# Products that need a normalised chunk, made inside the normalisation's own block

## The chip, the cores and the metric

The kernel runs on one core of one Trainium2 chip. The metric is the time of one execution in microseconds on the device. Before the change it is 1138.36 us, the median of 3 runs (1136.8 to 1141.94).

## The reference

Two layers work on 2048 tokens (64 batches of 32) of width 128, in float32, with a context of 64 x 257 rows of 128. All of it is one chain of residual sums:

```python
x = x + _L0_xattn_ref(_layernorm(x, axis=-1), ctx_1024, ctx_1024, mask_Bx1x1xS2_fk0, ...)
x = x + _L0_attn_ref(_layernorm(x, axis=-1), L0_attn_Wq, L0_attn_Wk, L0_attn_Wv, ...)
x = x + _L0_ffn_ref(_layernorm(x, axis=-1), L0_ffn_router_w, L0_ffn_router_b, ...)
x = x + _L1_xattn_ref(ctx_1024, _layernorm(x, axis=-1), mask_BxS2_bk0, L1_xattn_Wq, ...)
x = x + _L1_attn_ref(_layernorm(x, axis=-1), ...)
x = x + _L1_ffn_ref(_layernorm(x, axis=-1), ...)
```

`_layernorm` takes the mean and the variance over the 128 features and returns `(x - m) / sqrt(v + eps)`. The first four modules matter here: a cross attention of 16 heads to the context, a self attention with a memory term, a router that picks two of eight experts for each token, and a second cross attention (16 heads of 64) in which the latents are normalised again with an affine and stand beside the context as keys and values.

## The kernel before, in words

The tokens lie transposed in `xT` [128 features, 2048 tokens], the normalised ones in `yT`. The stages run one after the other in `perceiver`, and every stage consists of blocks (`nc.Block()`): in a block each engine has its own program, joined to the others by semaphores, and at the end of a block all engines wait for each other (in the trace `PEq L172` and the like: an engine that waited at the block's end).

`layernorm` (L168 to L225) works on four chunks of 512 tokens. PE makes the mean of a chunk with a matmul by a matrix of 1/128 (L193), DVE subtracts it (L204), ACT squares (L219), PE makes the variance (L196), ACT takes logarithm and exponential for the inverse root (L222, L225), DVE multiplies (L208) and, where there is an affine, applies it (L211). PE's program order is two means, then variances and means in turn, and at the end ten filler matmuls whose result nobody reads (`occupied(core, 0, 10)`, L56), which run while DVE and ACT finish the last chunks. The means are in PSUM banks 0 to 3, the variances in banks 4 to 7.

The four calls and what stands behind each:

- `cross_attention_0`, ln0. A block in which PE makes the queries of four chunks (L285) and a small product of the last context column (L287), DVE copies them out with bias and scale (L294, L297) and POOL builds a table of heads (L270 to L277). Then the loop's block, whose first instruction on SP loads context (L310).
- `memory_attention_0`, ln1. A block in which PE makes queries and keys of four chunks (L610), DVE copies the eight banks out (L624) and makes a gate (L627 to L631), and POOL fills and selects several tables (L586 to L595). Then the loop's block (POOL L685, L681, L682).
- `experts_0`, ln2, whose SP program also loads the experts' weights (`fetch`). In the block behind it PE makes the router's logits of 16 tiles of tokens into bank 0 (L1189) and transposes the tokens into rows in banks 4 to 7 (L1192); POOL first fills eight rank planes (L1115), and DVE's first step on the logits (L1365) waits for them and for the logits. ACT copies the rows out (L1294), SP loads context units (L1036) and then stores the rows (L1081), and POOL gathers from them much later (L1106).
- `cross_attention_1`, ln3 with an affine and the second epsilon. Behind it SP loads four masks (L1510), stores the latents' rows and, once these have landed, loads the rows of keys for the first two batches (L1518). PE transposes the latents (L1658), makes the queries of the first group of four batches (`queries(-1, ...)`, L1599), then waits for POOL's copy of the latents into the keys (L1565) and for DVE's rows of latents (L1768, `lat_kept`), and starts the loop. ACT copies the queries out (L1681).

The loop of `cross_attention_1` runs over 64 batches in 8 turns of 8; a batch is four units of four heads. For a unit PE makes scores into bank 0 or 1 (L1609), DVE adds the mask and takes the maximum (L1726), ACT the exponential (L1688), DVE the reciprocal of the sum (L1732), POOL multiplies by it (L1555), DVE transposes (L1740). Behind every second batch PE makes the means of two batches from the transposed probabilities and the rows of keys (L1622) in banks 2 to 5. The order on DVE is `maximum(u)`, `invert(u - 1)`, `turn(u - 2)`.

## Time and profile before

| what | value |
|---|---|
| median of 3 runs | 1138.36 us (1136.8 to 1141.94) |
| the profiled execution | 1137.78 us, its span 1135.5 us |
| PE, DVE, ACT, POOL busy | 1001.3, 738.2, 734.7, 485.9 us |
| mean granted TensorE clock | 0.964 |
| ln0, ln1, ln2, ln3 begin at | 8.88, 260.86, 383.66, 549.09 us |

The profile is of one execution, with times from its span's start. In a row of its timeline stand the start, the length, the engine, the line of the kernel, the operation with its tiles, and in brackets how long the engine stood idle before it and what ended that. Rows of one kind that follow each other are merged with their count, and a float32 matmul counts as two instructions. An engine's name with a q (SPq, POOLq) is its queue.

### The profile page before, as it was taken

The page shows a single profiled execution, that of the slowest core. Times are in us where ns is not written, and L with a number is a line of the kernel's source. Part 1 is how long each engine was busy: PE and PEld are TensorE (multiplying, and loading weights), DVE is VectorE, ACT ScalarE, POOL GpSimd, SP SyncE. Part 2 cuts the span into 40 slices and gives each one's busy share as a digit, 9 for nine tenths or more (in the row PEclk, how much of TensorE's full clock was granted, in tenths as well). Part 3 has the DMA queues.
Part 4 walks back from the last instruction along what each step waited for, and adds up shares of the span by engine and source line. Part 5 has one row for each costly group of instructions (what it writes and reads, how often), then busy time and mean ns, then how long its engine had stood idle before and what let it go on. Part 6 is the DMA issues. An engine that isn't in the chain of part 4 may idle for free. (4 is left out here: it accounts for less than half of the span.)

```text
span 1135.5 us, 37923 instructions
## 1 busy us (share of the span) xinstructions
PE 1001.3 (88%) x13868; PEld 793.3 (70%) x13868; DVE 738.2 (65%) x2792; ACT 734.7 (65%) x1794; POOL 485.9 (43%) x883
## 2 busy tenths in 40 slices
PE   5799999987688769998899999999999998878864
PEld 2678888873677459887678888888888887323343
DVE  3578888875789578995476556556556553473376
ACT  3578888873578528885376766766756754564467
POOL 1122222213655026675066666766666765102042
PEclk9899999999799889999999999999999999998979
DMA  2443333310000455773365445445455442000001
GB/s 61 115 115 78 83 81 77 83 39 1 1 1 2 159 189 187 233 226 99 97 154 144 119 114 144 114 117 137 118 126 133 112 123 68 29 0 0 1 0 38
DMA packets 70699, 105.57 MB, mean 93 GB/s; under 512 B 12560, under 2 KB 50320, under 8 KB 70384
## 3 DMA queue, kind: packets, MB, share of 16 engines
q1 hardware_dynamic: 68080, 98.84, 32.3%
q0 software_dynamic: 2496, 5.12, 1.7%
q8 instruction: 75, 1.23, 0.5%
q14 instruction: 48, 0.39, 0.1%
HBM read 89.12 MB, written 14.79 MB: 92 GB/s over the span
## 5 line engine op out<-in xcount | busy, mean ns | idle before, releaser
L1688 ACT ACTIVATE d_p<-d_p,d_nmax 128x289 f32<-128x289 f32 x256 | 137.1, 539 | 128.3 <-DVE d_nmax L1726 127.5
L1555 POOL TENSOR_TENSOR d_p<-d_p,d_rtotal 128x288 f32<-128x288 f32 x256 | 169.3, 667 | 39.6 <-DVE d_rtotal L1732 35.0
L1726 DVE CUSTOM_DVE_ANT_0 d_p<-bank,d_low 128x289 f32<-128x289 f32 x256 | 109.7, 429 | 79.7 <-PE bank L1609 78.3
L1609 PE MATMUL bank<-x_keyT,d_q 128*128 128x289 f32 x512 | 155.1, 420 | 3.5 <-DVE d_nmax L1726 2.1
L1622 PE MATMUL bank<-d_pT,d_xr 32*128 32x128 f32 x4608 | 137.9, 273 | 1.4 <-ACT rows_out L1697 0.9
L445 ACT ACTIVATE a_p<-a_p,a_nmax 128x257 f32<-128x257 f32 x256 | 116.2, 506 | 33.7 <-DVE a_nmax L482 31.9
L1622 PEld LDWEIGHTS bank<-d_pT,d_xr 32*128 32x128 f32 x4608 | 131.6, 187 | 6.3 <-issue 2.1
L1740 DVE STREAM_TRANSPOSE d_pT<-d_p 128x288 f32<-128x288 f32 x256 | 119.2, 465 | 22.1 <-POOL d_p L1555 19.7
L482 DVE CUSTOM_DVE_ANT_0 a_p<-bank,a_low 128x257 f32<-128x257 f32 x256 | 93.8, 422 | 28.0 <-PE bank L395 26.5
L1609 PEld LDWEIGHTS bank<-x_keyT,d_q 128*128 128x128 f32 x512 | 82.3, 190 | 35.1 <-DVE d_nmax L1726 23.6
L353 POOL TENSOR_TENSOR a_edge<-a_vlast,a_p 128x32 f32<-128x32 f32 x64 | 15.7, 246 | 178.0 <-ACT a_p L445 165.2
L452 ACT ACTIVATE a_pT<-bank 128x512 f32<-128x512 f32 x128 | 69.7, 594 | 21.1 <-PE bank L404 20.6
L1572 POOL TENSOR_TENSOR d_a<-rows_out 128x512 f32<-128x512 f32 x64 | 80.1, 1274 | 7.2 <-ACT rows_out L1697 6.6
L1732 DVE RECIPROCAL d_rtotal<-d_total 128x1 f32<-128x1 f32 x256 | 40.5, 158 | 52.1 <-ACT d_p L1688 52.1
L1635 PEld LDWEIGHTS bank<-d_a,x_wvo 128*128 128x128 f32 x512 | 66.2, 192 | 9.0 <-POOL d_a L1572 2.8
L1599 PEld LDWEIGHTS bank<-yT,x_wqk 128*128 128x128 f32 x512 | 66.7, 192 | 6.4
L1635 PE MATMUL bank<-d_a,x_wvo 128*128 128x128 f32 x512 | 67.0, 275 | 2.6 <-POOL d_a L1572 2.6
L404 PE MATMUL bank<-ident,a_p 128*128 128x128 f32 x512 | 68.1, 277 | 0.0
L1599 PE MATMUL bank<-yT,x_wqk 128*128 128x128 f32 x512 | 67.0, 275 | 0.0
L404 PEld LDWEIGHTS bank<-ident,a_p 128*128 128x128 f32 x512 | 61.3, 144 | 6.6 <-issue 0.2
L417 PEld LDWEIGHTS bank<-a_v,a_pT 128*32 128x32 f32 x4096 | 42.3, 111 | 23.4 <-ACT a_pT L452 21.6
L1264 ACT ACTIVATE c_hs<-bank,c_w 128x128 f32<-128x128 f32 x156 | 44.6, 368 | 14.7 <-PE bank L1166 13.9
(344 smaller groups left out, 2183.4 us busy)
## 6 DMA issues: line engine op xcount, KB each, us to landing
d_xr<-key_rows SPq DMA_DIRECT2D x256, 144.0 KB, 3.2
d_low<-mask_low SPq DMA_DIRECT2D x64, 144.5 KB, 3.8
a_ctT<-in_ctxT SPq DMA_DIRECT2D x64, 128.5 KB, 2.1
a_low<-mask_low SPq DMA_DIRECT2D x64, 128.5 KB, 3.0
c_ct<-in_ctx SPq DMA_DIRECT2D x32, 256.0 KB
key_rows<-c_ct SPq DMA_DIRECT2D x32, 256.0 KB, 2.3
c_w<-in_L_ffn_w SPq DMA_DIRECT2D x8, 578.0 KB, 10.3
c_w<-expert_out SPq DMA_DIRECT2D x8, 256.0 KB, 4.9
```

What stands on the lines that cost most here:

```text
L404: ins = nc.tensor.transpose(TP[k][:, 128 * g:128 * g + 128], P[:, r % 2, g, 128 * k:128 * k + 128], core.ident[:])
L445: nc.scalar.activation(P[:, r % 2, g, :], P[:, r % 2, g, :], ACT.Exp, bias=nmax[:, r % 2, g:g + 1], scale=-1.0).then_inc(exp_made, 1)
L482: nc.vector.tensor_tensor_reduce(P[:, r % 2, g, :], S[g], low[:, r % RING, :], -1.0, 3.4e38, ALU.add, ALU.min, accum_out=nmax[:, r % 2, g: ...
L1555: nc.gpsimd.tensor_tensor(p, p, rtotal[:, b % 2, g:g + 1].broadcast_to([128, EDGE]), ALU.mult).then_inc(normed, 1)
L1572: nc.gpsimd.tensor_tensor(a[:, n // 4 % 2, :, n % 4, :], context_part[:, n % 2].rearrange("p j (g q) -> p (j g) q", g=GROUPS), latent_part ...
L1599: ins = nc.tensor.matmul(Q[:, 128 * h:128 * h + 128], wqk[:, 4 * r + h, :], latT[:, bass.ds((i * 2 + ahead) * 128, 128)], start=True, stop ...
L1609: nc.tensor.matmul(S[u % 2], q[:, b // 4, b % 4, 4 * g:4 * g + 4, :].rearrange("p h q -> p (h q)"), keyT[:, bass.ds(i * EIGHT + b, 1), :]. ...
L1622: ins = nc.tensor.matmul((OL if latents else O)[n % 2][j], xr[rows, n % 2, k, :], pT[rows, n % 4, :, 32 * k:32 * k + 32], start=(k == 0 or ...
L1635: ins = nc.tensor.matmul(OUT, wvo[:, h, :], a[:, ago % 2, 4 * (h % 4) + h // 4].rearrange("p b q -> p (b q)"), start=(h == 0), stop=False)
L1688: nc.scalar.activation(p, p, ACT.Exp, bias=nmax[:, b % 2, g:g + 1], scale=-1.0, accum_out=total[:, b % 2, g:g + 1]).then_inc(exp_made, 1)
L1726: nc.vector.tensor_tensor_reduce(P[:, b % 2, g, 0:KEYS], S[u % 2], low[:, b % 4, :], -1.0, 3.4e38, ALU.add, ALU.min, accum_out=nmax[:, b % ...
L1740: nc.vector.transpose(pT[:, b % 4, g, :], P[:, b % 2, g, 0:EDGE]).then_inc(turned, 1)
```

## The change

`layernorm` gets two arguments. With `follow` the ten fillers are left out and PE calls `follow(pe, c)` for each chunk, once that chunk is scaled (L208) or, where `shaped` is given, once the affine is applied (L211). The four callers give it: the queries behind ln0 and ln1, for each chunk four router products and four transposes behind ln2, and behind ln3, with its first chunk, the 16 matmuls of the first group's queries, now into banks 0 to 3.

```diff
@@ -194,7 +194,15 @@
                 if s >= 1:
                     pe.wait_ge(squared, before + s)
                     nc.tensor.matmul(var[:, s - 1, :], core.mean_w[:], chunk(sq, s - 1), start=True, stop=True).then_inc(var_ready, 1)
-            occupied(core, 0, 10)
+            if follow is None:
+                occupied(core, 0, 10)
+            else:
+                for c in range(NCH):
+                    if shaped is None:
+                        pe.wait_ge(scaled, before + c + 1)
+                    else:
+                        pe.wait_ge(shaped, c + 1)
+                    follow(pe, c)
 
         @block.vector
...
@@ -230,7 +238,14 @@
     nc = core.nc
     DH, GROUPS, RING = D // HEADS, 4, 4
     QUADS = BATCH // RING
-    layernorm(core, "ln0", core.xT, core.yT)
+    q_made = core.sem("a_q_made")
+
+    def ask(pe, c):
+        if c == 0:
+            pe.wait_ge(core.weights.a_loaded, 128)
+        nc.tensor.matmul(core.bank[:, c, :], core.weights.a["wq"][:], chunk(core.yT, c), start=True, stop=True).then_inc(q_made, 1)
+
+    layernorm(core, "ln0", core.xT, core.yT, follow=ask)
     with ExitStack() as own:
         sb = lambda n, s, dt=F32: core.sb(n, s, dt, own)
         sem = core.stage_sem
...
@@ -280,9 +295,6 @@
 
             @block.tensor
             def _(pe):
-                pe.wait_ge(w.a_loaded, 128)
-                for c in range(NCH):
-                    nc.tensor.matmul(core.bank[:, c, :], wq[:], chunk(core.yT, c), start=True, stop=True).then_inc(q_made, 1)
                 pe.wait_ge(w.edge_loaded, 16)
                 nc.tensor.matmul(core.bank[0:BATCH, 4, 0:128], w.ctx_last[:], wv[:], start=True, stop=True).then_inc(vl_made, 1)
...
-                pe.wait_ge(w_loaded, 128)
-                for n, w in enumerate((wq, wk)):
-                    for c in range(NCH):
-                        nc.tensor.matmul(core.bank[:, n * NCH + c, :], w[:], chunk(core.yT, c), start=True, stop=True).then_inc(q_made, 1)
+                for c in range(NCH):
+                    nc.tensor.matmul(core.bank[:, NCH + c, :], wk[:], chunk(core.yT, c), start=True, stop=True).then_inc(q_made, 1)
 
             @block.vector
             def _(dve):
...
+        LG = core.bank[:, 0, 0:128]
+        logit_made, rows_turned = core.sem("c_logit_made"), core.sem("c_rows_turned")
+
+        def route(pe, c):
+            if c == 0:
+                pe.wait_ge(w_loaded, 176)
+            for m in range(4 * c, 4 * c + 4):
+                ins = nc.tensor.matmul(LG[:, E * m:E * m + E], core.yT[:, 128 * m:128 * m + 128], router[:], start=True, stop=True)
+            ins.then_inc(logit_made, 1)
+            for m in range(4):
+                ins = nc.tensor.transpose(core.bank[:, 4 + c, 128 * m:128 * m + 128], chunk(core.yT, c)[:, 128 * m:128 * m + 128], core.ident[:])
+            ins.then_inc(rows_turned, 1)
+
+        layernorm(core, "ln2", core.xT, core.yT, room=(flat[:, 0:TOK], flat[:, TOK:2 * TOK]), fetch=fetch, follow=route)
         sem = core.stage_sem
...
@@ -1184,14 +1214,6 @@
                     ins = nc.tensor.transpose(TC[u % 2][:, 128 * m:128 * m + rows], ct[0:rows, slot_of(u), m, :], core.ident[0:rows, 0:rows])
                 ins.then_inc(turned, 1)
 
-            pe.wait_ge(w_loaded, 176)
-            for m in range(TILES):
-                ins = nc.tensor.matmul(LG[:, E * m:E * m + E], core.yT[:, 128 * m:128 * m + 128], router[:], start=True, stop=True)
-            ins.then_inc(logit_made, 1)
-            for m in range(TILES):
-                ins = nc.tensor.transpose(core.bank[:, 4 + m // 4, 128 * (m % 4):128 * (m % 4) + 128], core.yT[:, 128 * m:128 * m + 128], core.ident[:])
-                if m % 4 == 3:
-                    ins.then_inc(rows_turned, 1)
             pe.wait_ge(prod_loaded, 64)
             pe.wait_ge(gate_step, 1)
             products(0, (wqT, wkT))
...
@@ -1359,7 +1381,7 @@
                                           ALU.subtract, ALU.mult)
                 ins.then_inc(centred, 1)
 
-            dve.wait_ge(logit_made, 1)
+            dve.wait_ge(logit_made, NCH)
...
-        layernorm(core, "ln3", core.xT, core.yT, affine[:, 2:3], affine[:, 3:4], twice=True)
+        q_made, shaped = core.sem("d_q_made"), core.sem("d_shaped")
+
+        def ask(pe, c):
+            if c == 0:
+                for r in range(4):
+                    for h in range(4):
+                        ins = nc.tensor.matmul(core.bank[:, r, 128 * h:128 * h + 128], wqk[:, 4 * r + h, :], core.yT[:, 0:128], start=True, stop=True)
+                    ins.then_inc(q_made, 1)
+
+        layernorm(core, "ln3", core.xT, core.yT, affine[:, 2:3], affine[:, 3:4], twice=True, follow=ask, shaped=shaped)
         latT, lat_rows = core.yT, core.out
 
```

In `cross_attention_1` the transposes of the latents move behind the first two scores, on DVE the rows of latents (L1768 before) behind the first two maxima, and the wait for them from the loop's start to the first means. POOL's copy of the latents into the keys comes in two parts, of the first 8 batches and of the other 56; PE waits for the second at the second turn.

```diff
-                nc.gpsimd.tensor_copy(keyT[:, :, CTX - 1:EDGE], latT[:].rearrange("p (b q) -> p b q", b=BATCH)).then_inc(latents_placed, 1)
+                for part in (slice(0, EIGHT), slice(EIGHT, BATCH)):
+                    nc.gpsimd.tensor_copy(keyT[:, part, CTX - 1:EDGE], latT[:].rearrange("p (b q) -> p b q", b=BATCH)[:, part]).then_inc(latents_placed, 1)
                 nc.gpsimd.memset(lasts[:], 0.0).then_inc(cleared, 1)
 
...
+                    if n == 0:
+                        pe.wait_ge(lat_kept, NCH)
                     if n % 2 == 0 and n >= 2:
                         pe.wait_ge(o_copied, 2 * n)
                     for k in range(BLOCKS):
...
+                def latent_rows():
+
+                    for m in range(TILES):
+                        ins = nc.tensor.transpose(core.bank[:, 2 + m // 4, 128 * (m % 4):128 * (m % 4) + 128], latT[:, 128 * m:128 * m + 128], core.ident[:])
+                        if m % 4 == 3:
+                            ins.then_inc(lat_turned, 1)
+
                 def body(i, first, last):
                     for b in range(EIGHT):
+                        if i == 1 and b == 0:
+                            pe.wait_ge(latents_placed, 2)
                         scores(i, b, 0, first)
                         scores(i, b, 1, first)
+                        if first and b == 0:
+                            latent_rows()
                         if not (last and b >= 4):
                             queries(i, b)
...
 
-                for m in range(TILES):
-                    ins = nc.tensor.transpose(core.bank[:, 2 + m // 4, 128 * (m % 4):128 * (m % 4) + 128], latT[:, 128 * m:128 * m + 128], core.ident[:])
-                    if m % 4 == 3:
-                        ins.then_inc(lat_turned, 1)
-                for r in range(4):
-                    queries(-1, 4 + r)
                 pe.wait_ge(latents_placed, 1)
-                pe.wait_ge(lat_kept, NCH)
                 unrolled(TURNS, body)
                 for r in range(3):
...
+                def latent_rows():
+
+                    for c in range(NCH):
+                        dve.wait_ge(lat_turned, c + 1)
+                        nc.vector.tensor_tensor(lat_rows[:, 4 * c:4 * c + 4, :], core.bank[:, 2 + c, :].rearrange("p (m d) -> p m d", m=4),
+                                                cx.media[:, 1, :].unsqueeze(1).broadcast_to([128, 4, 128]), ALU.subtract).then_inc(lat_kept, 1)
+
                 def body(i, first, last):
                     for u in range(UNITS):
                         b, g = divmod(u, GROUPS)
                         maximum(i, u, first)
+                        if first and u == 1:
+                            latent_rows()
                         if b % 4 == 0 and g == 1 and i * EIGHT + b >= 12:
                             project(i, (b - 12) // 4)
                         if not (first and u < 1):
```

PE's program from the last variances of ln0 to the first scores' block. The names: `ln_sq` the squares, `wa_wq` the query weights. Before:

```order
L196 MATMUL bank<-ln_sq,mean_w 128x512 x2
L56 MATMUL bank<-ident,mean_w 128x128 x10
L172 UNCONDITIONAL_BRANCH
L281 UNCONDITIONAL_BRANCH
L285 MATMUL bank<-yT,wa_wq 128x512 x4
L287 MATMUL bank<-wa_wv,wa_ctx_last 64x128
L266 UNCONDITIONAL_BRANCH
```

and now:

```order
L196 MATMUL bank<-ln_sq,mean_w 128x512 x2
L246 MATMUL bank<-yT,wa_wq 128x512 x4
L172 UNCONDITIONAL_BRANCH
L296 UNCONDITIONAL_BRANCH
L299 MATMUL bank<-wa_wv,wa_ctx_last 64x128
L281 UNCONDITIONAL_BRANCH
```

The fillers (L56) are gone and the four query products stand in their place, ahead of the block's end (L172); of the next block's PE program only the small product is left.

PE's program at the end of ln3 and the opening of the second cross attention; `x_wqk` are the query weights, `d_q` the queries, `x_keyT` the keys. Before:

```order
L196 MATMUL bank<-ln_sq,mean_w 128x512 x2
L56 MATMUL bank<-ident,mean_w 128x128 x10
L172 UNCONDITIONAL_BRANCH
L1589 UNCONDITIONAL_BRANCH
L1658 MATMUL bank<-ident,yT 128x128 x16
L1599 MATMUL bank<-yT,x_wqk 128x128 x16
L1609 MATMUL bank<-x_keyT,d_q 128x289 x2
L1599 MATMUL bank<-yT,x_wqk 128x128 x4
L1609 MATMUL bank<-x_keyT,d_q 128x289 x4
```

and now:

```order
L196 MATMUL bank<-ln_sq,mean_w 128x512 x2
L1504 MATMUL bank<-yT,x_wqk 128x128 x16
L172 UNCONDITIONAL_BRANCH
L1621 UNCONDITIONAL_BRANCH
L1638 MATMUL bank<-x_keyT,d_q 128x289 x2
L1676 MATMUL bank<-ident,yT 128x128 x16
L1628 MATMUL bank<-yT,x_wqk 128x128 x4
L1638 MATMUL bank<-x_keyT,d_q 128x289 x4
```

The 16 query matmuls (L1599, now L1504) moved ahead of the block's end, and the 16 transposes (L1658, now L1676) behind the first two scores.

DVE's program at the same place; `rows_out` holds the latents' rows, `d_p` the probabilities. Before:

```order
L1716 UNCONDITIONAL_BRANCH
L1768 TENSOR_TENSOR rows_out<-bank,x_media 128x512 x4
L1726 ISA d_p,d_nmax<-bank,d_low 128x289
L1726 ISA d_nmax 128x1
L1726 ISA d_p,d_nmax<-bank,d_low 128x289
L1726 ISA d_nmax 128x1
L1732 RECIPROCAL d_rtotal<-d_total 128x1
L1726 ISA d_p,d_nmax<-bank,d_low 128x289
L1726 ISA d_nmax 128x1
L1732 RECIPROCAL d_rtotal<-d_total 128x1
```

and now:

```order
L1751 UNCONDITIONAL_BRANCH
L1761 ISA d_p,d_nmax<-bank,d_low 128x289
L1761 ISA d_nmax 128x1
L1761 ISA d_p,d_nmax<-bank,d_low 128x289
L1761 ISA d_nmax 128x1
L1794 TENSOR_TENSOR rows_out<-bank,x_media 128x512 x4
L1767 RECIPROCAL d_rtotal<-d_total 128x1
L1761 ISA d_p,d_nmax<-bank,d_low 128x289
L1761 ISA d_nmax 128x1
L1767 RECIPROCAL d_rtotal<-d_total 128x1
```

The four steps on the latents' rows stand behind the first two maxima, ahead of the first reciprocal.

## Rows read from the trace of the kernel before

**Rows 1.** The profile's page, its span, then busy time of each engine (first section).

```profile
span 1135.5 us, 37923 instructions
...
PE 1001.3 (88%) x13868; PEld 793.3 (70%) x13868; DVE 738.2 (65%) x2792; ACT 734.7 (65%) x1794; POOL 485.9 (43%) x883
```

**Rows 2.** Timeline, end of ln0, query block, loop's start: start us, length us, engine, line, operation.

```profile
18.51 2.39 PE L56 MATMUL bank<-ident,mean_w 128*128 128x128 f32 x20
...
21.20 3.67 PE L285 MATMUL bank<-yT,wa_wq 128*128 128x512 f32 x8 [0.30 <-PEq L172]
...
22.41 3.25 DVE L294 TENSOR_SCALAR a_qT<-bank,wa_bias 128x512 f32<-128x512 f32 x4 [1.63 <-PE bank L285]
...
25.57 0.27 DVE L297 TENSOR_TENSOR a_vl<-bank,wa_bv 64x128 f32<-64x128 f32 x1
...
26.12 0.33 SPq L310 DMA_DIRECT2D a_ctT<-in_ctxT  x1
```

**Rows 3.** Instructions of line 294, DVE's copies of the queries: count, ns min/median/max.

```profile
L294 DVE TENSOR_SCALAR a_qT<-bank,wa_bias x4: 751/751/751, 22.4 to 24.9; 128x512 f32<-128x512 f32 x4
```

**Rows 4.** Timeline, the block behind ln1: POOL's tables, DVE's copies, the next block.

```profile
272.19 0.10 POOL L590 MEMSET b_own_head<- 128x4 f32 x1 [20.68 <-SPq L577]
...
272.47 0.31 DVE L620 COPY b_norm<-wb_norm_col 64x1 f32<-64x1 f32 x2
...
278.45 0.46 POOL L586 TENSOR_SCALAR_AFFINE_SELECT b_key_scale<-b_key_scale 128x4 f32<-128x4 f32 x2
...
280.48 0.15 DVE L631 TENSOR_SCALAR wb_gate<-wb_gate 128x1 f32<-128x1 f32 x1
...
280.90 0.95 POOL L685 MEMSET b_vb<- 128x1024 f32 x1 [1.99 <-POOLq L577]
```

**Rows 5.** Timeline, end of ln2 and the start of the router's block.

```profile
393.53 2.39 PE L56 MATMUL bank<-ident,mean_w 128*128 128x128 f32 x20
...
396.18 0.45 POOL L1115 MEMSET x_keyT<- 128x16 f32 x8 [32.61 <-POOLq L172]
...
399.78 1.94 PE L1192 MATMUL bank<-ident,yT 128*128 128x128 f32 x16
...
399.97 0.29 DVE L1365 TENSOR_TENSOR x_keyT<-bank,wc_router_b 128x128 f32<-128x128 f32 x1 [4.16 <-PE bank L1189]
```

**Rows 6.** Timeline, end of ln3 and the opening of the second cross attention.

```profile
557.80 2.39 PE L56 MATMUL bank<-ident,mean_w 128*128 128x128 f32 x20
...
560.92 3.35 SPq L1510 DMA_DIRECT2D d_low<-mask_low  x4
...
561.62 2.48 DVE L1768 TENSOR_TENSOR rows_out<-bank,x_media 128x512 f32<-128x512 f32 x4 [0.97 <-PE bank L1658]
...
562.73 3.74 PE L1599 MATMUL bank<-yT,x_wqk 128*128 128x128 f32 x32
...
566.50 0.60 ACT L1681 ACTIVATE d_q<-bank 128x512 f32<-128x512 f32 x1 [0.30 <-PE bank L1599]
...
567.24 1.21 PE L1609 MATMUL bank<-x_keyT,d_q 128*128 128x289 f32 x4 [0.78 <-ACT d_q L1681]
...
568.11 0.46 DVE L1726 CUSTOM_DVE_ANT_0 d_p<-bank,d_low 128x289 f32<-128x289 f32 x1 [4.00 <-PE bank L1609]
...
569.27 0.16 DVE L1732 RECIPROCAL d_rtotal<-d_total 128x1 f32<-128x1 f32 x1 [0.20 <-ACT d_p L1688]
...
570.44 0.46 DVE L1740 STREAM_TRANSPOSE d_pT<-d_p 128x288 f32<-128x288 f32 x1
...
581.07 4.30 PE L1622 MATMUL bank<-d_pT,d_xr 32*128 32x128 f32 x144
```

**Rows 7.** DMA issues of 560.5 to 561.0 us: count, KB each, median us to landing.

```profile
d_low<-mask_low SPq DMA_DIRECT2D x1, 144.5 KB, 3.8
```

**Rows 8.** Stretches of PE around 425 us: stretch, its length, PE busy (count), granted clock, DMA share, GB/s.

```profile
422.20:425.20 3.00, 0.39 (x2) 1.00 0.20 60
...
425.30:428.60 3.30, 3.30 (x17) 0.50 0.13 40
```

More of the change, by code:

```diff
@@ L210, in _ @@
                         dve.wait_ge(scaled, before + c + 1)
-                        nc.vector.tensor_scalar(chunk(dst, c), chunk(dst, c), gamma, beta, ALU.mult, ALU.add)
+                        nc.vector.tensor_scalar(chunk(dst, c), chunk(dst, c), gamma, beta, ALU.mult, ALU.add).then_inc(shaped, 1)
         @block.scalar
@@ L560, in memory_attention_0 @@
     GROUPS = BATCH // 4
-    layernorm(core, "ln1", core.xT, core.yT)
+    q_made = core.sem("b_q_made")
+    def ask(pe, c):
+        if c == 0:
+            pe.wait_ge(core.weights.b_loaded, 128)
+        nc.tensor.matmul(core.bank[:, c, :], core.weights.b["wq"][:], chunk(core.yT, c), start=True, stop=True).then_inc(q_made, 1)
+    layernorm(core, "ln1", core.xT, core.yT, follow=ask)
     with ExitStack() as own:
@@ L1679, in queries @@
                         act.wait_ge(s_made, (i * 2 + ahead - 1) * 4 * GROUPS)
-                    Q = FIRST_Q[r if i < 0 else 0]
+                    Q = core.bank[:, r, :] if i < 0 else NEXT_Q
                     nc.scalar.activation(q[:, ahead % 2, :, 4 * r:4 * r + 4, :].rearrange("p b h q -> p h b q"),
@@ L1764, in body @@
                             turn(i, u - 2, first)
-                for c in range(NCH):
-                    dve.wait_ge(lat_turned, c + 1)
-                    nc.vector.tensor_tensor(lat_rows[:, 4 * c:4 * c + 4, :], core.bank[:, 2 + c, :].rearrange("p (m d) -> p m d", m=4),
-                                            cx.media[:, 1, :].unsqueeze(1).broadcast_to([128, 4, 128]), ALU.subtract).then_inc(lat_kept, 1)
                 unrolled(TURNS, body)
```

26 lines of the change are left out of this document (12 added, 14 removed).

## The prediction

> **What bounds the kernel now.** I began with the page: a span of 1135.5 us in which PE is busy for 1001.3 us and no other engine for more than 740 [rows 1]. The busy share says little here, since the change touches only four short stretches, each at the end of a normalisation, where stages are closed off by blocks in which every engine waits for the last. So I read the timeline there. In each the reader should look for the engine that ends the block, and for what the block behind it waits for.
>
> Behind ln0, PE's ten fillers end at 18.51 + 2.39 = 20.90 and its first query product starts at 21.20: a block opens 0.3 us after its last engine. The four products take 3.67 us, DVE's copies follow each at PE's pace (22.41 to 25.66), the small sum ends at 25.84, and SP's first load of the loop goes out at 26.12 [rows 2]. Behind ln1, DVE ends at 280.63 and the next block opens at 280.90, while POOL had built its tables from 272.19 to 278.91 [rows 4]. Behind ln2, POOL's ranks run from 396.18 to 396.63 and DVE's first step on the logits waits for the router until 399.97 [rows 5]. Behind ln3, transposes of the latents, then four groups of queries (3.74 us), then ACT's last copy, ending at 567.10, release the first scores at 567.24 and DVE's first maximum at 568.11 [rows 6].
>
> **The change, part by part.** In all four places the moved products take the place of the fillers (2.39 us) and start when those did. They are longer than the fillers, so PE now ends the normalisation's block. What is saved is not the products' time but what remains of it after the later opening and the next engine's own work.
>
> *Query products behind ln0.* They run from 18.51 to 18.51 + 3.67 = 22.18, the next block opens at 22.48 in place of 21.20. DVE then finds all four banks full. Its copies go by its own pace: one lasts 0.751 us [rows 3], but the sum behind the last starts 0.66 us after it (25.57 against a last copy that starts at 25.66 - 0.75 = 24.91) [rows 2, 3]. Four at 0.66 and the sum of 0.27 end at 22.51 + 2.64 + 0.27 = 25.42, and SP's load, 0.28 later, goes out at 25.70 where it did at 26.12: 0.4 us gained. All that the loop starts with (key loads, the last values' round trip) stands behind this opening and moves with it.
>
> Weighed against that row: the pace of copies. The rows give 0.66 between starts for a copy of 0.75. The Trainium skill, page "VectorE: DVE Perf Modes", section "The DRAIN you can't avoid", says that the next operation doesn't start until the pipe is empty. By it the copies would take 4 x 0.75 = 3.0 us and the gain would be about 0.1; the trace doesn't agree for this pair, so I keep 0.4, with 0.1 as the lower end.
>
> *Query products behind ln1.* The block opens at 269.54 + 3.67 + 0.26 = 273.47, which is 1.28 later (269.54 is where PE's fillers begin, 2.39 + 0.26 before the 272.19 of the row) [rows 2, 4]. PE has only the key products left (another 3.67, ending at 277.2), DVE starts to copy at 273.47 + 0.6 (its small copies end at 272.78) and needs eight copies. The nearest row for a copy without a wait is 2.48 us for four [rows 6], so eight end by 279.0, and the three gate steps by 279.6. POOL, however, starts its 6.72 us (272.19 to 278.91) 1.28 later too, ends at 280.19, and becomes the engine that opens the next block, at 280.46 in place of 280.90: 0.4 us gained. If a copy took 0.75, DVE would end at 280.6 and nothing would be gained. That is the lower end; the upper is 0.5.
>
> *Router and rows behind ln2.* 16 router products and 16 transposes take from the block's opening at 396.2 to 399.78 + 1.94 = 401.72, 5.5 us [rows 5]. From 393.53 they end at 399.03, and the block opens at 399.3, 3.1 later than before. The logits are then ready, but the first step also waits for POOL's eight rank fills, which now start at 399.3 and take 0.45 [rows 5]. So DVE starts at 399.8 in place of 399.97: 0.15 us. Behind that lies DVE's own chain of small steps; ACT's row copies, the products of weights and the count of chosen experts move with it or sit idle beside it. Queued later by 3.1 us are SP's seven loads and then its four stores of rows; the gathers of POOL, which need these stores, come behind DVE's whole chain, so I cost this at nothing. If that cover were gone, up to 3.1 us would be lost.
>
> *First group behind ln3.* The queries end at 557.80 + 3.74 = 561.54, the block opens at 561.80, 0.9 later than 560.92. ACT has four copies of 0.60 at most and ends by 564.2, so the scores start at 564.35, nearly 3 us earlier, and DVE could follow 0.87 behind, at 565.2 [rows 6]. Here other waits take over. The first mask lands 3.8 us after its issue [rows 7], and its issue moved with the block: 561.80 + 3.8 = 565.6. Two maxima take about 1 us (0.46 each and their reads). Then DVE does the latents' rows, which lay in the shadow of the queries before: 2.48 us, now in line, to 569.1. The reciprocal and, 1.17 us behind it by way of POOL (570.44 - 569.27), the first transpose come at 570.3, against 570.44 [rows 6]. PE on its side has the scores (1.2), the transposes (1.9) and a group of queries (0.9) before the third score: 568.4, and 0.87 more for DVE, 569.3, so both engines arrive together. With nothing else this gives 0.2 us, and not 3.
>
> And PE now stands idle from 561.54 to 564.35, where before it waited 0.8. After 3.0 us in which it had 0.39 us of work its granted clock was 0.50, that is 1.2 in place of 2.4 GHz, for the 3.3 us of work that followed [rows 8]. With the fillers gone nothing prevents that here. Half of 3.3 us is a delay of 1.65 on PE's side; against the 570.44 of before that makes up to 1.0 us lost. The Trainium skill, page "TensorE: Matmul & The Clock Gate", section "HAM oscillation — how this bites in real kernels", says in the same sense that waits within a stream of matmuls can leave the array at half rate. The row and that rule point the same way, against this part of the change. Between +0.2 and -1.0 I take -0.3, nearer to the end without it since a part of the slow work lies under the wait for the mask.
>
> The latents' stores go out about 2.9 us later, the last at 569.1. The first means ran at 581.07 [rows 6]. From 569.1 to there lie 12 us for two landings, of the stores and of the rows loaded back, at some 3.8 us each by the nearest row [rows 7], and the issue of eight loads between them (3.35 us for four masks [rows 6], so at most 6.7). That fits with little to spare if the issues are slow, and easily if they are not; costed at nothing, at up to 2.3 us in the worst case (569.1 + 3.8 + 6.7 + 3.8 = 583.4).
>
> **Sum.** 0.4 + 0.4 + 0.15 - 0.3 = 0.65 to 0.8, with the roundings. The profiled execution took 1137.78 us around its span of 1135.5; less 0.8 it would be 1137.0. The median of the runs is 1138.36, 0.6 above it, so about 1137.6 there. I give 1137.5. A measurement of this kernel can tell about 0.5% (5.7 us) from no change, and this is far below.
>
> **Rivals.**
> 1. *All that is moved is saved.* If the shorter chains passed straight on, 3.67 + 3.67 + 5.5 + 3.74 + 1.94 = 18.5 us would go, and the time would be 1120. For it speaks that each product does stand alone on PE between two blocks; against it, the later opening of each block (1.3, 1.3, 3.1 and 0.9) and POOL's and DVE's own work behind it. Chance 0.03.
> 2. *The opening of the last stage gains in full.* If the mask lands early, the clock holds and DVE's rows of latents fit between its maxima, nearly 3 us come there: 1138.36 - 0.95 - 2.9 = 1134.5. Against it: DVE's 2.48 us are in its program order. Chance 0.09.
> 3. *Slower: the clock stays low through the opening of that stage.* From 564.35 on PE has two scores, 16 transposes, eight query matmuls and two scores (1.2 + 1.9 + 0.9 + 1.2 = 5.2 us). If all of it runs at half rate, 5.2 us are added, of which the earlier start covers about 0.5, and 0.95 is gained elsewhere: 3.7 slower, 1142. It decides from the point at which PE's delay exceeds DVE's arrival at 569.3. For it speaks rows 8; against it that the slow stretch there ended after 3.3 us of steady work. Chance 0.10.
> 4. *The change doesn't do what it says*, because the products wait for the last chunk anyway: then PE ends later by the products' whole length, about as before, 1138.4. The third chunk is scaled before PE comes to it, so this is unlikely: 0.04.
>
> **Chances.** The forecast has 0.70; 0.04 is left for something unseen in either direction. Faster by over 0.5% comes from rival 1 and a part of rival 2 and of the unseen: 0.06. Slower by over 0.5% from the far end of rival 3 and the unseen: 0.05. The rest, 0.89, lies within 0.5%. The range reaches from 1134.2 (rival 2) to 1141.2 (most of rival 3, and the spread of the runs, 1136.8 to 1141.94).
>
> **What would show it.** Right: fillers gone behind the four normalisations, SP's first load at about 25.7, POOL's last table as the end of the block behind ln1, DVE's first logit step waiting for POOL, and DVE's first maximum in the last attention at about 565.6 released by a mask's DMA, the first transpose within 1 us of where it was. Wrong: a first transpose 2 us or more ahead, a wait of POOL's gathers for the rows' stores, or a wait of the first means for their rows.

## The result, and the profile after

The changed kernel takes 1130.78 us (median of 6 runs, 1127.38 to 1131.78) against 1138.05 of the kernel before in the same comparison (6 runs, 1136.8 to 1141.94). The ratio is 0.9925, with a 95% interval of 0.9907 to 0.9942: faster by 7.3 us, where I forecast less than 1 and a range that ended 3.4 us above this. The page after, as [rows 1]:

```profile
span 1129.5 us, 37765 instructions
...
PE 997.1 (88%) x13788; PEld 789.1 (70%) x13788; DVE 736.7 (65%) x2792; ACT 734.6 (65%) x1794; POOL 487.8 (43%) x884
```

PE lost 80 products and 80 weight loads, the four sets of fillers, and 4 us of busy time. The four places that the prediction worked out, from the timeline of the changed kernel (start us, length us, engine, line, operation). The loop's start behind ln0, as [rows 2]:

```profile
18.61 3.60 PE L246 MATMUL bank<-yT,wa_wq 128*128 128x512 f32 x8
...
22.61 2.73 DVE L306 TENSOR_SCALAR a_qT<-bank,wa_bias 128x512 f32<-128x512 f32 x4 [1.72 <-PEq L172]
25.25 0.27 DVE L309 TENSOR_TENSOR a_vl<-bank,wa_bv 64x128 f32<-64x128 f32 x1
25.79 0.33 SPq L322 DMA_DIRECT2D a_ctT<-in_ctxT  x1
```

Four copies from 22.61 and the sum at 25.25, SP's load at 25.79: forecast 25.70, was 26.12. The block behind ln1, as [rows 4]:

```profile
268.14 1.88 PE L578 MATMUL bank<-yT,wb_wq 128*128 128x512 f32 x4
...
276.19 0.15 DVE L648 TENSOR_SCALAR wb_gate<-wb_gate 128x1 f32<-128x1 f32 x1
276.57 0.45 POOL L605 TENSOR_SCALAR_AFFINE_SELECT b_key_scale<-b_key_scale 128x4 f32<-128x4 f32 x2
277.33 0.95 POOL L702 MEMSET b_vb<- 128x1024 f32 x1 [0.31 <-POOLq L596]
```

DVE's gate ends at 276.34 and POOL's last table at 277.02, so POOL opens the next block, as forecast. From the first subtraction of ln1 to that memset the kernel before took 18.91 us, this one 18.46: 0.45 gained, forecast 0.44. The router's block, as [rows 5]:

```profile
389.78 0.95 PE L1071 MATMUL bank<-wc_router,yT 128*128 128x8 f32 x8
...
394.43 0.63 PE L1074 MATMUL bank<-ident,yT 128*128 128x128 f32 x4
...
395.35 0.45 POOL L1145 MEMSET x_keyT<- 128x16 f32 x8 [35.32 <-POOLq L172]
...
395.94 0.29 DVE L1387 TENSOR_TENSOR x_keyT<-bank,wc_router_b 128x128 f32<-128x128 f32 x1 [3.88 <-POOL x_keyT L1145]
```

DVE's first step on the logits is released by POOL's rank fills, as forecast. And the opening of the second cross attention, as [rows 6]:

```profile
552.00 3.73 PE L1504 MATMUL bank<-yT,x_wqk 128*128 128x128 f32 x32
...
556.02 1.77 SPq L1541 DMA_DIRECT2D d_low<-mask_low  x4
...
558.25 1.81 PE L1638 MATMUL bank<-x_keyT,d_q 128*128 128x289 f32 x4 [2.51 <-ACT d_q L1716]
559.23 0.46 DVE L1761 CUSTOM_DVE_ANT_0 d_p<-bank,d_low 128x289 f32<-128x289 f32 x1 [4.37 <-PE bank L1638]
...
559.85 3.03 PE L1676 MATMUL bank<-ident,yT 128*128 128x128 f32 x16
...
561.80 1.97 DVE L1794 TENSOR_TENSOR rows_out<-bank,x_media 128x512 f32<-128x512 f32 x3 [0.16 <-PE bank L1676]
...
564.87 0.46 DVE L1775 STREAM_TRANSPOSE d_pT<-d_p 128x288 f32<-128x288 f32 x1
```

Scores 1.81 where they took 1.21, transposes 3.03 where 1.91 (in a kernel below): PE runs at half clock here, after 2.51 us idle. From ln3's first subtraction to this transpose it is 20.43 us against 20.22 before: 0.2 lost, forecast 0.3.

So the four openings came out nearly as the prediction has them, and are worth less than 1 us together. Where are the 7.3? (The two profiled executions differ by 6.1 us, their spans being 1135.5 and 1129.5.) I set the two traces side by side by landmarks; a batch's row is the start of DVE's last step on that batch, the product that writes its output row. The changed kernel is ahead by 0.15 at the first loop's row of batch 4, by 3.39 at that of batch 6, by 3.12 at ln1, 4.03 when the experts' table is found, 5.45 at the first load of the experts' parts, 5.57 at the first transpose of the last stage. Most of it lies *between* the openings. In the kernel before, PE's timeline in the first loop shows:

```profile
59.98 0.72 PE L395 MATMUL bank<-a_kT,a_qb 32*128 32x257 f32 x8
60.66 0.71 PE L417 MATMUL bank<-a_v,a_pT 128*32 128x9 f32 x64
62.82 0.67 PE L376 MATMUL bank<-a_ctT,wa_wk 128*128 128x257 f32 x2 [1.45 <-issue]
63.33 1.83 PE L404 MATMUL bank<-ident,a_p 128*128 128x128 f32 x8
```

and its stretches (length, busy us of PE, PEld, DVE, ACT, POOL with counts, granted clock, DMA share, GB/s):

```profile
62.00:63.40 1.40, 0.58 (x3) 0.50 (x4) 0.53 (x3) 0.20 (x1) 0.00 (x0) 1.00 0.59 73
63.40:66.80 3.40, 3.40 (x21) 2.84 (x19) 1.19 (x4) 1.99 (x4) 0.04 (x1) 0.50 0.06 13
```

Ahead of the ninth key product PE stands for 1.45 us with nothing that the profile shows it to wait for ("issue"), and then runs 3.4 us at clock 0.50. What the product needs was there 2 us earlier: its context landed at 58.99 us and DVE's copy of the keys before it ended at 59.26, while the gap runs from 61.37 to 62.82. The changed kernel at the same work:

```profile
59.62 0.72 PE L407 MATMUL bank<-a_kT,a_qb 32*128 32x257 f32 x8
60.30 0.71 PE L429 MATMUL bank<-a_v,a_pT 128*32 128x9 f32 x64
61.05 0.67 PE L388 MATMUL bank<-a_ctT,wa_wk 128*128 128x257 f32 x2
61.56 1.04 PE L416 MATMUL bank<-ident,a_p 128*128 128x128 f32 x8
```

No gap, and transposes at 1.04 in place of 1.83. Nothing in this loop was edited. What differs, beside an opening that is 0.3 us earlier, is where its instructions stand in PE's stream: the trace has the ten fillers as 20 products and 20 weight loads, so the loop comes 40 instructions sooner.

### The profile page after: what moved, and what is told of

Its sections match the earlier page's. It is cut to its first block and busy times, and to the rows that moved or that the text cites. A ratio compares the mean times of both kernels' runs of the same rounds, so it can differ in the third digit from the quotient of the medians.

```text
span 1129.5 us, 37765 instructions
## 1 busy us (share of the span) xinstructions
PE 997.1 (88%) x13788; PEld 789.1 (70%) x13788; DVE 736.7 (65%) x2792; ACT 734.6 (65%) x1794; POOL 487.8 (43%) x884
## 5 line engine op out<-in xcount | busy, mean ns | idle before, releaser
L1628 PEld LDWEIGHTS bank<-yT,x_wqk 128*128 128x128 f32 x480 | 62.9, 192 | 6.3
L1628 PE MATMUL bank<-yT,x_wqk 128*128 128x128 f32 x480 | 63.2, 275 | 0.0
## 6 DMA issues: line engine op xcount, KB each, us to landing
c_w<-in_L_ffn_w SPq DMA_DIRECT2D x8, 578.0 KB, 10.6
```

Of the source, the lines that this page charges most:

```text
L1628: ins = nc.tensor.matmul(NEXT_Q[:, 128 * h:128 * h + 128], wqk[:, 4 * r + h, :], latT[:, bass.ds((i * 2 + ahead) * 128, 128)], start=True, ...
```

## The experiments

Theory A: the gain that I did not forecast comes from the place of PE's code, and from clock levels that follow. Theory B: it comes from the moved products. All runs are compared with the kernel before on the same chip; there are four comparisons, each on a chip of its own, and the median of the kernel before was 1140.6, 1140.0, 1140.2 and 1157.7 us in them.

**The kernel before again, and parts alone.** `before_again` is the kernel before, unedited. `only_ln0`, `only_ln1`, `only_ln2` and `only_ln3` hold the change's edits at one normalisation each:

```
-    layernorm(core, "ln0", core.xT, core.yT)
+    layernorm(core, "ln0", core.xT, core.yT, follow=ask)
```

> The kernel before, unchanged, for a second profile. In its first profile DVE stored its sixth and seventh output row of the first attention's loop 1.3 and 3.2 us later than the changed kernel did, behind an idle time of PE of 1.45 us at 61.4 us that the profile puts down to issue, and a granted clock of 0.5 from 63.4. Theory A (the gap belongs to the program: the same instruction is late in every run): an idle time of over 1 us by issue before the same key matmul (L376), 1.4 to 1.5 us long. Theory B (the gap was chance): none there. Time: ratio 1.000 within 0.003 in either case.

> The change behind ln0 alone: fillers out, queries in. Theory A (PE's code lies 40 instructions earlier in its stream, which moves or hides the late instruction at 61 us): the opening gains 0.4 us, the loop another 2.5 to 3, total 2.9 to 3.5 us, about 1134.8. Theory B (chance): only 0.4 us, 1137.6. My forecast's sum said 0.4.

> The change behind ln3 alone. By the profile after, the first transpose of the last attention comes 0.2 us later than it would without this part, so I expect 0.0 to 0.5 us slower, 1138.1 to 1138.6. Rival: the part is worth the 3 us by which its scores start earlier: 1135.

> The change behind ln1 alone. My sum: 0.4 us faster, with POOL's tables as the end of the block; the opening from ln1's first subtraction to POOL's first fill of the next block goes from 18.90 to 18.46 us. If theory A holds, PE's code behind it is moved by 40 instructions as well, and a gain of over 1 us in the total would be from elsewhere in the program.

> The change behind ln2 alone. My sum: 0.15 us faster (DVE's first step on the logits waits for POOL's rank fills). From ln2's first subtraction to that step: 14.23 us before, 14.66 in the profile of the changed kernel, whose clock was low at other times, so between 14.0 and 14.7 here. Rival: the longer block delays the context loads and the stores of rows, and POOL's gathers wait: over 1 us slower.

Measured: 1.0002 (0.9982 to 1.0022) for the unedited kernel; 0.9958 (0.9940 to 0.9975), 0.9961 (0.9937 to 0.9985), 0.9933 (0.9907 to 0.9958) and 0.9966 (0.9946 to 0.9987) for ln0, ln1, ln2, ln3. The parts add up to 1.8%, the whole is 0.8%: what each gains is not all its own. Three of the expectations missed: only_ln1, only_ln2 and only_ln3 were to give 0.4, 0.15 and at most 0 us, and gave 4.5, 7.6 and 3.9. The unedited kernel has its gap again, 1.72 us:

```profile
64.52 0.67 PE L376 MATMUL bank<-a_ctT,wa_wk 128*128 128x257 f32 x2 [1.72 <-issue]
```

**The place of PE's code.** `after_pad40` puts 40 empty PE instructions at the changed kernel's start. The trace has none of them (37765 instructions, as without them), and where they should have run, PE's next recorded step follows 0.10 us after the one ahead of it in both kernels. So I take this run as the changed kernel once more and not as a test of the place; had they been there, it would speak against theory A, since the gap did not come back. `before_nofill0` is the kernel before without ln0's ten fillers (the first edit below), `before_half0` has five of them; `after_fill` and `before_fill10` have ten more ahead of the first loop (the second edit):

```
-            occupied(core, 0, 10)
+            if name != "ln0":
+                occupied(core, 0, 10)
```

```
+                occupied(core, 5, 10)
                 keys(0, 0, True)
```

> The changed kernel with 40 empty instructions on PE in the set-up block, where PE is idle until 8.8 us anyway, so that the loop's code stands where it stood before the change in PE's stream. Theory A (place in the stream): the late instruction at about 61 us is back, and with it up to 3 us: 1133.5. Theory B (the earlier opening, or chance): same as the changed kernel, 1130.8 within 1.

> The kernel before without the ten fillers behind ln0 and nothing else. The opening should be the same within 0.1 us (DVE ends ln0 at 20.78, the fillers at 20.90). Theory A (PE's code for the loop lies 40 instructions earlier, which takes away the wait by issue before the ninth key matmul, L376, and the slow clock behind it): 3 to 4 us faster than before, and the row of batch 6 comes 6.7 us behind that of batch 4 in place of 9.9 and 10.2. Theory B (the earlier opening or the products themselves do it): same as before within 1 us, 9.9 us between these rows.

> The changed kernel with ten fillers on PE at the start of the first loop's block, ahead of the first key matmul, where PE waits some 5 us for the context anyway: the loop's code is where it was before the change. Theory A: the wait before the ninth key matmul is back (9.5 us or more between the rows of batches 4 and 6), less what the kept clock gives; 1 to 3 us slower than the changed kernel, about 1132.5. Theory B: 6.7 us between these rows, 1130 or a little less.

> The kernel before with ten more 128-column products on TensorE ahead of the first key product of the first loop's block, which do nothing for the result: TensorE's later instructions stand 40 places further on in its stream. Theory A (TensorE stops in the first loop where its stream happens to reach code that has not come in, and the place of the code decides where): the 1.45 us without work ahead of the ninth key product goes or moves, batch 4's row to batch 6's takes 6.7 to 8 us in place of 9.9 or 10.2, last scatter to first load of parts 2.4 in place of 3.7, and the kernel is 2 to 5 us faster for added work, near 1136. Theory B (what the change saved there is a matter of the products that were moved): both stretches as before, 1140 us or more by the products' 1 us.

> The kernel before with five in place of ten filling products in the first normalisation: TensorE's code 20 instructions nearer. The gap ahead of the ninth key product was 0.8 to 1.7 us in all eight kernels with that code at its old place or 40 further on, and absent in all six with it 40 nearer. If the loop's code comes in a fixed time and TensorE runs into it, the gap shrinks gradually (0.3 to 0.9 us here); if the place alone decides (a boundary that the code crosses), it is whole or gone. Time between 1137.5 and 1140.

Measured: 0.9922 (0.9895 to 0.9948), 0.9978 (0.9957 to 0.9999), 0.9927 (0.9900 to 0.9954), 0.9991 (0.9974 to 1.0008), 0.9957 (0.9940 to 0.9973). The kernels of this study in order of where the loop stands, with the time from batch 4's row to batch 6's:

| place of the loop in PE's stream | kernels | gap near the ninth key product | batch 4's row to 6's, us |
|---|---|---|---|
| 40 instructions further on | before_fill10 | 1.43 | 9.94 |
| as before | before, before_again, only_ln1, only_ln2, only_ln3, before_nofill2, after_fill | 0.80 to 1.72 | 7.38 to 10.19 |
| 20 nearer | before_half0 | none | 6.56 |
| 40 nearer | changed kernel (3 profiles), before_nofill0, only_ln0, but_ln2, ln2_nofill0, after_warm3, after_warm10 | none | 6.57 to 6.88 |

Theory A holds for this stretch: the gap is there or not by the place alone, and whether the query products were moved is of no account. The times say less: before_nofill0 gained 2.5 us with an interval from 0.1 to 4.9, and after_fill, which has the gap back and 7.93 us in this stretch, cannot be told from the changed kernel. I had expected that a shift the other way would remove the gap too and make the kernel 2 to 5 us faster. It did neither, and how it did not is the best evidence. PE in before_fill10:

```profile
60.81 0.55 PE L417 MATMUL bank<-a_v,a_pT 128*32 128x9 f32 x44
62.79 0.36 PE L417 MATMUL bank<-a_v,a_pT 128*32 128x9 f32 x20 [1.43 <-issue]
63.10 1.21 PE L376 MATMUL bank<-a_ctT,wa_wk 128*128 128x257 f32 x2
```

The gap now lies 20 products ahead of the key product, which with their weight loads is 40 instructions: the shift. By a count of PE's recorded products and weight loads from the start, it lies behind 1220 of them in the kernels where it precedes the key product, behind 1218 here and behind 1217 in after_fill, where it precedes the last product of the output. In both of these it stands inside a group of products that has no wait, so it is no wait for data. It sits at one place of the stream, whatever work stands there, and only on the first pass through the loop's code: the 13 passes after it show none. before_half0 says that it does not shrink gradually.

The gap alone costs 0.8 to 1.7 us. In before, before_again and before_fill10 a stretch of 3.4 us at clock 0.50 follows before batch 6's row, and these three take 9.91 to 10.19 us; in the other five with a gap none does, and they take 7.38 to 8.30.

That the engine waits there for code is an inference. For it speaks that packets of kind "instruction", 16 KB each, come every 5 to 8 us there, and that in all eight kernels the gap ends 2.48 to 2.74 us after the start of such a packet, though its length differs by 0.9 us. What remains open is why it is gone at 20 and 40 nearer, where the same place of the stream should lie within the loop too, and where such a packet comes at the same time (60.12 us in both profiles shown above).

The second place is the end of the experts: from POOL's last scatter to SP's first load of the parts. In the kernel before, the DMA view of 531.7 to 535.4 us (kind with its packets, MB, share of the engines; then issues, with median us to landing):

```profile
q8 instruction: 1, 0.02, 1.9%
issues: line engine op xcount, KB each, median us to landing
expert_out<-rows_out,c_row_at POOLq DMA_INDIRECT x1, 3.5
```

and of only_ln2 from 531.5 to 533.9 us, with no such packet:

```profile
q0 software_dynamic: 64, 0.13, 16.0%
issues: line engine op xcount, KB each, median us to landing
c_w<-expert_out SPq DMA_DIRECT2D x1, 256.0 KB, 2.9
expert_out<-rows_out,c_row_at POOLq DMA_INDIRECT x1, 2.2
```

In the four kernels with PE's code here at its old place or further on (before, before_again, only_ln3, before_fill10) an instruction packet falls into the scatter's flight, and the stretch takes 3.68 to 4.06 us; in the other fourteen profiles there is none, and it takes 2.38. That is 1.4 us by the means for PE's code being shorter. It also explains why the parts add up to more than the whole: only_ln0, only_ln1 and only_ln2 each have it. That the packet is what delays the scatter is argued from this agreement and not tested by itself.

**The router.** `before_nofill2` drops only ln2's fillers (the edit below), `but_ln2` is the changed kernel with the router left in its own block, `ln2_nofill0` is only_ln2 with ln0's fillers dropped too.

```
-            occupied(core, 0, 10)
+            if name != "ln2":
+                occupied(core, 0, 10)
```

> The kernel before without the ten products that fill the third normalisation (40 instructions fewer from the router on, nothing moved in the first loop). Theory A (place of code): the stretch of batch 4's row to batch 6's stays at 9.9 to 10.2 us, last scatter to first load of parts falls from 3.7 to 2.4, and the time by some 1 us, to 1139. The router's block: if its 3 us in four of six profiles hang on the clock alone and not on the fillers, third normalisation to experts found stays at 32.9 or 35.9. If the fillers were what kept it, it takes 35.9 or more, and the time rises to 1140 or 1141.

> The changed kernel with the router and the rows left in their own block as before (queries of both attentions and the last opening as changed). If the router's part is worth what it measured alone (0.67%, which would hold some of the place of code), this is near 1134 us; if it is worth the mean of the profiles (35 against 33.3 us, and no more, since the place of code is given by the other parts), 1132; if it is worth what I forecast by the profile of before (0.15 us), 1131. Third normalisation to experts found: 32.9 or 35.9, against 33.3 in the changed kernel.

> The router's part of the change alone, and the kernel before's first normalisation without its ten filling products (TensorE's code 40 instructions nearer, no query product moved). My account of the result so far: place of code in the first loop (batch 4's row to batch 6's 6.7 us, no gap ahead of the ninth key product), router's block (third normalisation to experts found 33.3 to 34.0), last scatter to first load 2.4; and these make most of the change's gain. Then this kernel lacks only the openings' 0.3 and 0.45 us and stands within 1.5 us of the changed kernel, 1131 to 1133. Rival (the gain needs the query products inside the normalisations): 1135 or more.

> The changed kernel again, unedited, so that the other three and it are compared on one chip, and to see which of its stretches repeat. All theories: 0.991 to 0.994 of before; batch 4's row to batch 6's 6.7 us, third normalisation to experts found 33.3 to 34.0, last scatter to first load 2.4, fourth normalisation to first transpose 20.4.

Measured: 0.9977 (0.9958 to 0.9995), 0.9980 (0.9961 to 0.9999), 0.9941 (0.9920 to 0.9962), and 0.9922 (0.9899 to 0.9945) for the changed kernel again. From ln2's first subtraction to the experts' table, the ten profiles with the old router show 32.84 and 32.85 (twice) and 35.46 to 36.26 (eight times); the eight with the new one 33.24 to 34.02. The old one in before_again:

```profile
397.69 5.14 PE L1189 MATMUL bank<-wc_router,yT 128*128 128x8 f32 x32 [0.30 <-PEq L172]
402.69 3.65 PE L1192 MATMUL bank<-ident,yT 128*128 128x128 f32 x16
402.87 0.29 DVE L1365 TENSOR_TENSOR x_keyT<-bank,wc_router_b 128x128 f32<-128x128 f32 x1 [5.60 <-PE bank L1189]
```

and its stretches:

```profile
395.00:399.70 4.70, 4.40 (x39) 4.24 (x38) 1.38 (x2) 1.52 (x3) 1.88 (x17) 1.00 1.02 415
399.70:406.50 6.80, 6.80 (x34) 6.47 (x35) 3.25 (x12) 1.91 (x4) 0.18 (x1) 0.50 1.02 410
```

Here the clock fell to 0.50 although PE had been busy for 4.40 of the 4.70 us before; 32 products took 5.14 us and 16 transposes 3.65 where [rows 5] has 1.94. All eight slow profiles of the old router have such a stretch, 6.8 to 6.9 us at 0.50 that begin 12.1 to 13.6 us behind ln2's first subtraction; the two quick ones are at full clock there, and the profile I predicted from was one of these. The new router is nearly indifferent, since three quarters of its products are made beside DVE's chunks and PE is through with all of them 13.8 us behind the subtraction in the changed kernel: after_warm3 and after_warm10 have the same slow stretch and take 33.46 and 33.43. In after_pad40 the clock is 0.50 for 13.7 us, from before the router's block until well into it, and it still takes 34.02:

```profile
379.01:413.04 34.03, 25.29 (x164) 19.09 (x164) 21.99 (x45) 14.62 (x22) 4.42 (x18) 0.70 0.74 275
390.00:403.70 13.70, 11.65 (x83) 10.65 (x84) 7.32 (x28) 4.00 (x6) 2.08 (x17) 0.50 1.05 389
```

By the means (35.36 and 33.44) this part is worth 1.9 us. The times give it more: but_ln2, which has all of the change except this part, took 1136.64 us where the expectations were 1131 to 1134. It keeps 2.3 us of the gain, so some 6.6 us of the whole hang on the router's part (0.9980 against 0.9922, in different comparisons). ln2_nofill0, on the other hand, comes near to the whole with no query product moved: 0.9941 of the kernel before against 0.9922, 1.8 us apart where I expected up to 1.5, and less than the intervals can separate.

**The opening of the last stage.** `after_warm3` and `after_warm10` put twenty and ten fillers where PE idles ahead of the first scores. The edit of after_warm10; after_warm3 has 20 in place of its 10:

```
+                occupied(core, 7, 10)
                 pe.wait_ge(latents_placed, 1)
                 unrolled(TURNS, body)
```

> The changed kernel with twenty 128-column products (2.3 us, no use in the result) on TensorE between the query products and the first scores of the second cross attention, where it idles 2.5 us. Theory C (the last opening lost its gain to the clock that fell to 0.5 over the latent rows' transposes): fourth normalisation to the first transpose of probabilities takes 19.3 us in place of 20.4, as where the part stood alone, and the kernel is 1 us faster, near 1130. Rival: the clock falls all the same, since the profile shows low stretches at places with TensorE busy too, and nothing changes.

> The changed kernel with ten filling products, not twenty, ahead of the second cross attention's first scores. Twenty took 4.70 us where 2.5 were idle: the clock stayed full, and the first scores came at 559.84 in place of 558.25. Ten take 2.35 us and end before the queries' copies do. Theory C: clock full and no delay, so fourth normalisation to first transpose 19.3 us in place of 20.4, and a kernel 1 us under the changed one in the same comparison. Rival: 20.4 as in the changed kernel, and no difference.

Measured: 0.9939 (0.9920 to 0.9959) and 0.9914 (0.9892 to 0.9937). My 2.3 us for twenty fillers was wrong by two, since each is two products: they took 4.70 us and pushed the scores out, and ln3 to the first transpose took 21.24. Ten do what was meant:

```profile
576.19 2.47 PE L56 MATMUL bank<-ident,mean_w 128*128 128x128 f32 x20 [0.32 <-PEq L172]
...
578.49 1.14 PE L1638 MATMUL bank<-x_keyT,d_q 128*128 128x289 f32 x4
579.47 1.91 PE L1676 MATMUL bank<-ident,yT 128*128 128x128 f32 x16
579.57 0.46 DVE L1762 CUSTOM_DVE_ANT_0 d_p<-bank,d_low 128x289 f32<-128x289 f32 x1 [4.58 <-DMA d_low<-mask_low]
...
583.73 0.48 DVE L1776 STREAM_TRANSPOSE d_pT<-d_p 128x288 f32<-128x288 f32 x1 [0.28 <-POOL d_p L1586]
```

The clock holds, and the opening takes 19.17 us in place of 20.43; the first maximum is now released by the mask, which in the changed kernel was hidden behind the slow scores. So the clock costs 1.26 us there. only_ln3, without such fillers, kept its clock and took 19.29 after the same 2.51 us idle; why the clock held in it alone is open. Against the changed kernel on the same chip after_warm10 is 1.4 us faster by the medians (1147.25 and 1148.69), as the profiles say, but the intervals overlap. It is the best candidate and not shown to be better.

## Why the prediction was wrong

Point by point, by the means of the 18 profiles with and without each thing (the second column is of all kernels that are there as the kernel before is; the last row leaves out only_ln3, with 19.29, and the two kernels with fillers in that place):

| stretch, us | without | with | gained | forecast |
|---|---|---|---|---|
| ln0 to SP's first load | 15.34 | 15.25 | 0.1 | 0.4 |
| batch 4's row to 6's (place of code) | 8.67 | 6.74 | 1.9 | none |
| ln1 to the next block | 18.91 | 18.45 | 0.46 | 0.44 |
| ln2 to the experts' table | 35.36 | 33.44 | 1.9 | 0.15 |
| last scatter to first load (place of code) | 3.81 | 2.38 | 1.4 | none |
| ln3 to the first transpose | 20.22 | 20.43 | -0.2 | -0.3 |
| sum | | | 5.6 | 0.65 to 0.8 |

**The step that failed** is a sentence of the prediction's part on ln0, "all that the loop starts with ... moves with it", which the sum extends to the whole kernel: four openings were costed, and everything between them was taken to move rigidly. I had counted the ten fillers by their 2.39 us and not as 40 instructions in PE's stream. The row of the gap was in the trace, 1.45 us of "issue" followed by 3.4 us at clock 0.50, and also the scatter's landing at 3.5 us; neither was looked for, since no edited line stood there. The runs show 1.9 and 1.4 us at these two places in its stead.

**The second failure**, and by the times the larger, is the size of the router's term: 0.15 us in the sum, 1.9 by the profiles and up to some 6.6 by but_ln2. Within the one profile I had, it was nearly right in kind: DVE waits for POOL, and against that profile the part even lost (logits 14.66 us behind ln2 against 14.23; PE's work with its gaps ended 0.5 later than summed). But the profile was one of the two quick ones among the ten with the old router. [rows 8] had told me that the clock falls in this region; I used it against the change at ln3 and did not ask what it does to the chain that the change takes off PE's path.

**Right**: the ln1 opening to 0.01 us, with POOL as its end; ln3's, with the clock at half as [rows 8] suggested, though its first maximum waited for PE and not for the mask; DVE's pace of copies, where the changed kernel's four took 2.73 us to the end, about 0.66 apart, and not the 3.0 of a pipe emptied each time; no gather waited for the rows' stores and no first mean for its rows. The gain at ln0 is in the profile above (0.33) but not in the means: SP's first load came 15.16 and 15.95 us behind ln0 in the two profiles of the kernel before, and 14.74 to 15.94 with the change, so 0.3 is less than this place varies.

Rival 1 stays as far off as it was argued to be. Rival 2 (1134.5) is nearer in number but by another way: its opening never gained more than 1.05 us, even with a full clock.

**What is not placed.** The sum by means is 5.6 us, and the interval of the ratio asks for 6.6 to 10.6. For the kernels without the new router the named stretches and the measurement agree within the intervals (before_nofill0 3.3 named, 2.5 measured; before_half0 3.3 and 5.0; before_nofill2 1.4 and 2.6; before_fill10 0 and 1.0; but_ln2 3.7 and 2.3; only_ln0 3.4 and 4.8; only_ln1 1.9 and 4.5), except for only_ln3 (0.9 and 3.9, its interval 1.5 to 6.2). Of those with it, ln2_nofill0 agrees (5.2 and 6.8), while only_ln2 has 3.3 named and 7.6 measured, with an interval from 4.8, and the changed kernel falls short each time. So 1.6 (ln2_nofill0) to 4.7 us (but_ln2 against the changed kernel) more come with the router's part and lie in no stretch that repeats; their cause stays open. The stretches that vary from profile to profile (batch 0's row to batch 1's 3.24 to 5.38 us, batch 62's row to ln1 9.72 to 12.72, last transpose of probabilities to the end 185.2 to 191.3) are the place to look, but 18 single profiles don't show whether they differ.

## What to carry to other kernels

Cost an edit also as instructions taken from or put into an engine's stream, and look along the whole trace for idle time that ends in "issue" with the engine's inputs long ready: such a gap can come and go with any edit ahead of it, and here it went by dropping ten fillers. The word alone does not tell: 15 of the 18 profiles have another gap of 0.76 to 1.31 us by "issue" in the experts, always ahead of the same transpose of gathered rows whatever the shift, and most gaps of that line end by a gather's landing. It took a shift of the code to tell the two kinds apart. Before a stretch is priced from one profile, ask at which clock it ran; a chain of short products on the path is worth the mean over both levels, and taking it off the path made this kernel nearly indifferent to the level. And a part measured alone holds the effect of its place too: a control kernel that shifts the code without the edit belongs beside it.

## What was unexpected of the hardware

PE stopped for 0.80 to 1.72 us at one place of its stream, in the middle of a group of like products if need be. The Trainium skill, page "Trainium Architecture — The Big Picture", section "The software stack", has the instruction streams brought to each engine when the kernel is loaded. By these traces that is not the whole of it: packets of kind "instruction" run through the execution (in the first profile 76 of 16 KB, from 41.7 to 1136.8 us, and 55 of 8 KB), and one of them beside a scatter went with 1.4 us more. On the fourth comparison's chip the stretch in which DVE normalises the experts stage's context rows took 104.6 to 105.9 us where the other chips had 87.8 to 88.2, so absolute times of the comparisons are not to be mixed.
